# Moving weight clips between VectorE and GpSimd, and shortening a residual product, in a three-block transformer kernel

## What is computed

```python
x = x + xattn(layernorm(x), ctx_512, ...)        # 16 heads over 4096 keys
x = x + attn(layernorm(x), ln_w, ln_b, W_in, W_out)   # 16 heads of 32, adds its own input too
x = x + ffn(layernorm(x), w1, w2, w3)

def act_quant(x):
    scale = 127.0 / clip(max(abs(x), axis=-1), EPS)
    return clip(round(x * scale), -128.0, 127.0) / scale
def weight_quant(w):
    scale = 1.0 / clip(mean(abs(w)), EPS)
    return clip(round(w * scale), -1.0, 1.0) / scale
ffn(x) = bitlinear(silu(bitlinear(x, w1)) * bitlinear(x, w3), w2)
```

## Time and profile before

| what | value |
|---|---|
| time, three runs | 555.12, 554.95, 554.63 us (median 554.95) |
| the profiled execution | 555.15 us, span 553.4 us |
| mean granted TensorE clock | 0.997 |
| PE busy | 526.5 us, 95% of the span |
| DVE busy | 450.5 us, 81% |
| ACT busy | 364.7 us, 66% |
| POOL busy | 148.7 us, 27% |

### The profile page before, as it was taken

One profiled execution on the slowest core, in us unless ns is written; L12 is line 12 of the kernel. 1 busy time (PEld: TensorE's weight loads), 2 busy tenths in 40 slices (PEclk: granted clock), 3 DMA queues, 4 the chain that ended last, 5 costly groups with the idle time before them and its releaser, 6 DMA issues.

```text
span 553.4 us, 10020 instructions
## 1 busy us (share of the span) xinstructions
PE 526.5 (95%) x3831; PEld 353.1 (64%) x3835; DVE 450.5 (81%) x650; ACT 364.7 (66%) x445; POOL 148.7 (27%) x202
## 2 busy tenths in 40 slices
PE   6989998799999999999999999999998899998996
PEld 3757763367666666767666676766677686454543
DVE  3354995999999999999999999999998833569686
ACT  2124535887887787788788688688688614995442
POOL 2367953002202202202202202202100001596500
PEclk9999999899999999999999999999999999999999
DMA  8999288999999999999999999999999987700001
GB/s 305 350 358 306 106 141 261 232 205 184 209 191 205 199 197 198 211 212 204 207 204 195 202 205 195 199 207 196 203 191 197 153 333 277 322 0 1 1 2 38
DMA packets 288350, 107.93 MB, mean 195 GB/s; under 512 B 276928, under 2 KB 278464, under 8 KB 286912
## 3 DMA queue, kind: packets, MB, share of 16 engines
q1 hardware_dynamic: 288320, 107.54, 89.6%
HBM read 37.79 MB, written 0.52 MB: 69 GB/s over the span
## 4 chain that ended last, share of the span: by engine, by line
PE 78%; DVE 10%; ACT 5%; DMA 4%; issue 2%; SPq 1%; ACTq 0%; DVEq 0%
PE ps L679 19%; PE ps L681 9%; PE ps L661 9%; PE ps L662 9%; PE ps L663 9%; PE ps L711 4%; PE ps L722 3%; DMA keys<-ctxT 2%; DVE rows L1300 2%; PE ps L788 2%; PE ps L733 2%; DVE split L1272 2%; PE ps L629 1%; PE ps L631 1%; PE ps L630 1%
## 5 line engine op out<-in xcount | busy, mean ns | idle before, releaser
L679 PE MATMUL ps<-pT,VH 128*128 128x256 f16 x1024 | 195.7, 273 | 3.7 <-DMA pT<-split 3.7
L681 PE MATMUL ps<-pT,VL 128*128 128x128 f16 x1024 | 182.6, 219 | 0.0
L1300 DVE TENSOR_SCALAR_CACHE_REDUCE rows<-ps,qback 128x1024 f32<-128x1024 f32 x128 | 163.6, 1280 | 17.8 <-PE ps L663 17.4
L1052 ACT ACTIVATE split<-rows,rz 128x2048 f16<-128x2048 f32 x64 | 124.6, 1995 | 67.7 <-DVE rz L1240 67.6
L1272 DVE SCALAR_TENSOR_TENSOR split<-rows,rz,split 128x2048 f16<-128x2048 f32 x64 | 150.1, 2348 | 2.9 <-ACT split L1052 2.1
L679 PEld LDWEIGHTS ps<-pT,VH 128*128 128x128 f16 x1024 | 100.4, 98 | 44.0 <-DMA pT<-split 5.7
L1038 ACT ACTIVATE rows<-rows,negm 128x2048 f32<-128x2048 f32 x64 | 127.2, 1988 | 0.2 <-DVE negm L1305 0.2
L681 PEld LDWEIGHTS ps<-pT,VL 128*128 128x128 f16 x1024 | 100.4, 98 | 27.3 <-issue 0.4
L542 POOL TENSOR_TENSOR ctx_c<-acc 128x128 f32<-128x128 f32 x32 | 23.9, 748 | 296.5 <-ACT acc L1027 296.5
L661 PE MATMUL ps<-KH,qcur 128*128 128x512 f16 x256 | 97.5, 381 | 3.3 <-DVE rows L1300 3.3
L662 PE MATMUL ps<-KL,qcur 128*128 128x512 f16 x256 | 97.5, 381 | 0.0
(11 more groups left out here) (187 smaller groups left out, 622.7 us busy)
## 6 DMA issues: line engine op xcount, KB each, us to landing
w_sb<-w SPq DMA_DIRECT2D x3, 2816.0 KB, 15.6
wq_sb<-wq SPq DMA_DIRECT2D x4, 1024.0 KB, 8.1
wo_sb<-wo SPq DMA_DIRECT2D x16, 256.0 KB, 5.3
wkcq_sb<-wkcq SPq DMA_DIRECT2D x4, 768.0 KB, 9.7
keys<-ctxT SPq DMA_DIRECT2D x8, 256.0 KB, 8.6
stage<-ctxT SPq DMA_DIRECT2D x16, 128.0 KB, 9.0
stage<-kcos SPq DMA_DIRECT2D x8, 256.0 KB, 9.1
stage<-ksin SPq DMA_DIRECT2D x8, 256.0 KB, 9.6
```

Of the source, the lines that this page charges most:

```text
L679: nc.tensor.matmul(bank(6 + r % 2, 0, 256), VH[:, 4 * b + k, :], p.rearrange("p x q -> p (x q)"), start=(b == 0 and k == 0), stop=False)
L681: last = nc.tensor.matmul(bank(6 + r % 2, 0, 128), VL[:, 4 * b + k, :], p[:, 0, :], start=False, stop=(b == 7 and k == 3))
L1052: nc.scalar.activation(split[:, split_slot(r, half), :, 0, :], rows[:, k, half * 2048:(half + 1) * 2048].rearrange("p (b k) -> p b k", k=1 ...
L1300: nc.vector.tensor_scalar(rows[:, k, c * 1024:(c + 1) * 1024], ps[:, score_bank(s) * 512:(score_bank(s) + 2) * 512], qback[:, r // 2:r // ...
```

## The change

Four edits. (1) w1's clip becomes four instructions of 1408 columns on VectorE, at v = 2 to 5; w3's stays whole and moves to v = 5, behind the second `context_out`; w2's goes to GpSimd in eight pieces behind its rounding. (2) GpSimd's gate ahead of w2's passes goes. (3) The ten dummy products behind the output projection go. (4) x is split, by GpSimd, into x2hi (rounded to fp32r) and x2lo (the remainder, rounded too), and the float32 product with the identity becomes two fp32r products.

```diff
+    CLIPS = (4, 1)
...
+        x2hi = at("x2hi", A + 22 * KB, [128, TT, DM], f32r)
+        x2lo = at("x2lo", A + 26 * KB, [128, TT, DM], f32r)
+        identr = at("identr", A + 30 * KB, [128, 128], f32r)
...
                 nc.gpsimd.tensor_tensor(x_sb[:, t, :], x_sb[:, t, :], h1[:, t, :], ALU.add).then_inc(x2_done, 1)
+                if t == 0:
+                    nc.gpsimd.tensor_copy(identr[:, :], ident[:, :]).then_inc(identr_done, 1)
+                pool.wait_ge(x2_done, t + 1)
+                nc.gpsimd.tensor_copy(x2hi[:, t, :], x_sb[:, t, :]).then_inc(x2hi_done, 1)
+                pool.wait_ge(x2hi_done, t + 1)
+                nc.gpsimd.tensor_tensor(x2lo[:, t, :], x_sb[:, t, :], x2hi[:, t, :].bitcast(f32), ALU.subtract)\
+                    .then_inc(x2lo_done, 1)
...
             weight_round(1, w3_sb, w3b)
-            pool.wait_ge(wclip_done, 2)
             weight_magic(2, w2_sb)
             weight_round(2, w2_sb, w2b)
+            for k in range(WPIECES):
+                part = slice(k * DK * FF // WPIECES, (k + 1) * DK * FF // WPIECES)
+                pool.wait_ge(wround_done, WPIECES * 2 + k + 1)
+                nc.gpsimd.tensor_scalar(w2b[:, part], w2b[:, part], 1.0, -1.0, ALU.min, ALU.max).then_inc(w2clip_done, 1)
...
             for t in range(TT):
-                pe.wait_ge(x2_done, t + 1)
-                nc.tensor.matmul(bank(6 + t), ident[:, :], x_sb[:, t, :], start=True, stop=False)
+                pe.wait_ge(identr_done, 1)
+                pe.wait_ge(x2lo_done, t + 1)
+                nc.tensor.matmul(bank(6 + t), identr[:, :], x2hi[:, t, :], start=True, stop=False)
+                nc.tensor.matmul(bank(6 + t), identr[:, :], x2lo[:, t, :], start=False, stop=False)
...
-            keep_busy(10, 2)
             quantised_transposes(0)
...
                     if t == 0:
-                        pe.wait_ge(wclip_done, j + 1)
+                        pe.wait_ge(wclip_done[j], CLIPS[j])
...
-                    pe.wait_ge(wclip_done, 3)
+                    pe.wait_ge(w2clip_done, WPIECES)
...
-            def clip(j, wb):
+            def clip(j, wb, k):
                 dve.wait_ge(wround_done, WPIECES * (j + 1))
-                nc.vector.tensor_scalar(wb[:, :], wb[:, :], 1.0, -1.0, ALU.min, ALU.max).then_inc(wclip_done, 1)
+                part = slice(k * DK * FF // CLIPS[j], (k + 1) * DK * FF // CLIPS[j])
+                nc.vector.tensor_scalar(wb[:, part], wb[:, part], 1.0, -1.0, ALU.min, ALU.max).then_inc(wclip_done[j], 1)
...
-                if v in (2, 3):
-                    clip(v - 2, (w1b, w3b)[v - 2])
+                if v in (2, 3, 4, 5):
+                    clip(0, w1b, v - 2)
                 if v in (3, 5, 7):
                     context_out(v // 2 - 1)
+                if v == 5:
+                    clip(1, w3b, 0)
             context_out(FG - 1)
-            clip(2, w2b)
```

More of the change, by code:

```diff
@@ L291, in program @@
         warm_done = sem("warm_done")
-        wclip_done = sem("wclip_done")
+        wclip_done = [sem(f"wclip_done{k}") for k in range(2)]
+        w2clip_done = sem("w2clip_done")
+        identr_done = sem("identr_done")
+        x2hi_done = sem("x2hi_done")
+        x2lo_done = sem("x2lo_done")
         win_in = sem("win_in")
```

## The result

The changed kernel takes 572.89 us (median of six executions, 572.32 to 574.54), the kernel before beside it 555.29: a ratio of 1.0317 [1.0297, 1.0337]. The forecast was 551.7, and the time lies 1.9 us above the range's upper end. What happened is the rival "any unbroken GpSimd stream shuts VectorE out", priced there at 570.

The account below looks back on a forecast made before the run. VectorE's order of work in the last attention, then TensorE's queue, was taken to bound the kernel. Terms 1.7 + 0.5 + 1.45 - 0.4 = 3.25 off 554.95 gave 551.7; range 550 to 571, the forecast's own 550 to 553.

Parts of the forecast that it names:

- any unbroken GpSimd stream shuts VectorE out: Rival at w1's first quarter, 500.15: it stands until GpSimd's queue is dry, 520.7; 570 us; chance 0.25.
- the price of a quarter: w1's clip quarters, last attention: each waits for one GpSimd piece's remainder, 0.4 on average, 0.83 at most.
- The rounding pass alone: Rival at w3's clip: only GpSimd's rounding pass shuts VectorE out, clip ends at 517.7; 553.3 us; chance 0.14.
- Attention, gain 1.7: Last attention: the third context can begin at 514.6 instead of 516.35; gain 1.7, bounds none and 2.7.
- Residual, gain 0.5: Output projection, first tile: two fp32r products take 0.5 instead of one fp32 product's 1.06; gain 0.5.
- Dummies, gain 1.45: Behind the output projection: without dummies the transposes wait for h2b alone, 527.39 instead of 528.84; gain 1.45.
- GpSimd's clip piece, 0.75: GpSimd's clips of w2: 0.75 us a piece, 6.0 for eight, hidden behind the up projection.
- Given back, 0.4: Layernorm on VectorE: its tensor_scalar can wait for a GpSimd piece; loss 0.4, bounds 0 to 0.75.
- the clock falls: Rival at h2b's transposes: without dummies TensorE idles some 1.9, its clock falls, up to 2.8 more; 554; chance 0.07.

Follow-up runs that it names:

- turns: Changed kernel, but GpSimd waits for VectorE's four quarters and w3's clip in turn, and for both h2b before w2's fourth clip piece: 551.92 us, 0.9925.
- drained pieces: Changed kernel, but each GpSimd piece from w3's rounding on waits for the piece before it to have finished: 555.85 us, 0.9989.
- six touches: Changed kernel plus six two-column VectorE products between 485 and 497 us: median 559.13 us, 1.0061; profiled execution 551.11.

## Why the prediction was wrong, point by point

- **The step that failed** is the price of a quarter: "I take one piece's remainder: 0.4 on average, 0.83 at most". It measured 20.89. The step took the rows at 478.71 and 51.43 for the rule and the clip of 3.44 us for a peculiarity of the rounding pass: the walk let the first quarter wait only until w3's rounding was over (502.11), and took the change of pass for an opening. Three changes of pass went by. Both kinds of row were right; what told them apart was how long GpSimd had been running alone, 3 pieces at 478.71 and 19 at 500.15. The prediction had both bounds in hand, "nothing" and "the rest of GpSimd's stream", and chose by the nearest operation, not by the nearest state: the slow clip was the same instruction at the same time of the same stream.
- The Trainium skill, page "SBUF — State Buffer", section "Who interferes with whom", lets the second to issue block until the first has finished. The traces agree for a stream that is young or was lately held up (0.89 at 478.71; 0.54 to 1.17 behind a wait). They differ for an old one: 27 GpSimd instructions, 26 of them issued behind the quarter, went ahead of it.
- **The rival "shut out"** had place, mechanism and end right: the stream was to run dry at 520.7 (520.85 measured) and the quarter to end at 521.0 (521.23). Its price of the clock was too small. It allowed 0.6; eight transposes twice and eight scores alone took 1.94 + 1.97 + 2.08 = 5.99 rather than 1.11 + 1.12 + 1.06 (eight scores at full clock, at 497.53) = 3.29, 2.7 more, and the last context came 19.57 late, not 17.4 less the 1.1 for w3's clip.
- **The rounding pass alone** as the cause fell: a rounding pass begun behind a stop was open, and the multiplication of w2 was closed.
- **Attention, gain 1.7:** masked here. Where the quarters do get in, it shows: with turns the last context came 2.1 earlier, with the one wait ahead of w3's rounding 2.5 (54.99 behind the mark).
- **Residual, gain 0.5:** the two products take 0.50 and 0.39 and overlap. GpSimd's added work is hidden in 7.08 us of idle time as predicted, of which 3.90 are left. But the term left out that VectorE's clip of w2, which ended at 522.48, would have held the layernorm: with that clip in place 0.17 shows, with it gone, as in the changed kernel, 0.34 or 0.35.
- **Dummies, gain 1.45:** right, 1.39 in the changed kernel and 1.36 alone, and no fall of the clock behind it, with 1.03 us of idle time in front of the transposes (the fall of before had come behind 2.00). The Trainium skill's page "TensorE: Matmul & The Clock Gate", section "Why this matters for your kernels", warns of idle gaps between bursts; the traces agree, in that 18.52 us here and 2.59 us with a wait between pieces were each followed by half the clock; 2.33 us with one wait ahead of each pass were not.
- **GpSimd's clip piece, 0.75:** 5.93 / 8 = 0.74.
- **Given back, 0.4:** not seen here, as GpSimd was done before the layernorm. Where the quarters got in, it was more than the bound of 0.75: 1.6 with drained pieces and 1.2 with the one wait ahead of w3's rounding (6.03 us from the layernorm's start to h2b instead of 4.82). There TensorE then stood 2.23 us ahead of the transposes, and the granted clock was 0.72 from 526 to 532 us: the rival "the clock falls". Its price had been summed wrongly too: 551.7 and up to 2.8 is 554.5, not 554.
- **The rest of the forecast** about held once GpSimd stopped for 0.1 us: 0.9948 measured in that kernel, 551.7 / 554.95 = 0.9941 forecast. That is in part luck, since attention gained more than its term and the clips gave back more than theirs.

## What to carry to other kernels

A wait that keeps GpSimd still may be what lets VectorE at SBUF at all: before taking one away, look in the trace for a VectorE instruction that stands near the end of a long GpSimd stream, and price the change by that row and not by one from the stream's beginning. Look at the kind as well: tensor_scalar, tensor_tensor and scalar_tensor_tensor stood here, a one-column reciprocal did not. Where both engines must work side by side, break GpSimd's stream on purpose, with a wait on its own last piece every pass, or with waits that put its pauses where VectorE's instructions fall due; the latter also kept GpSimd's clips out of the layernorm (4.83 us to h2b instead of 6.03). A trace that shows an engine busier with less to do is showing a wait inside an instruction.

## What the runs showed of the hardware that I had not expected

- GpSimd's boundaries close to VectorE as its stream goes on undisturbed: open up to 7 pieces and at 12, partly at 13, closed at 15 and 19 (but for the one execution with six touches), for each tensor_scalar, tensor_tensor and scalar_tensor_tensor that was put there (20.45 to 21.89 us of standing where the changed kernel's stream was whole). A one-column reciprocal took 0.16 us 17 pieces on.
- A two-column product gets in without lengthening any GpSimd piece (0.47 at 495.00), and leaves the stream as closed as it was (the next quarter stood 20.80).
- One stop of GpSimd is enough: 0.1 us between w3's multiplication and its rounding took the kernel from 572.89 (1.0317 of the kernel before) to 553.32 (0.9948).
